# Causal attention: sums over tokens with whole fp32 probabilities, projected after the sum

## The reference

```python
x = _L0_conv_ref(x, ...)                       # attention without mask, added to x
t = _to_tokens(x)                              # (4, 1024, 64)
t = t + _L1_attn_ref(_ln_t(t), ...)            # causal attention, 8 heads of width 64
t = t + _L1_ffn_ref(_ln_t(t), ...)             # batch norm and a recurrence over tokens

def _L1_attn_ref(x, Wq, Wk, Wv, Wo):
    ...
    scores = jnp.einsum('bhqd,bhkd->bhqk', q, k) / D ** 0.5
    scores = jnp.where(causal[None, None], NEG_INF, scores)
    attn = jax.nn.softmax(scores, axis=-1)
    out = jnp.einsum('bhqk,bhkd->bhqd', attn, v)
    out = out.transpose(0, 2, 1, 3).reshape(B, N, H * D)
    return out @ Wo
```

## Time and profile before

| | |
|---|---|
| median of 3 runs | 571.24 us |
| the runs | 571.98, 571.24, 567.42 us |
| span of the profiled execution, first to last instruction | 567.0 us |
| mean granted TensorE clock | 0.974 of full speed |

### The profile page before, as it was taken

How to read it: one execution, slowest core, us unless ns; L and a number is a source line. 1 busy time by engine, 2 the same in 40 slices (tenths; PEclk the granted TensorE clock), 3 DMA queues, 4 the chain that set the end, 5 groups by cost and what they waited for, 6 DMA issues and landing times.

```text
span 567.0 us, 16744 instructions
## 1 busy us (share of the span) xinstructions
PE 490.0 (86%) x6771; PEld 323.0 (57%) x6771; DVE 398.8 (70%) x909; ACT 429.3 (76%) x832; POOL 424.4 (75%) x463
## 2 busy tenths in 40 slices
PE   4699978988799998889999988998999999787783
PEld 1277655655565755565666756565666766564431
DVE  5878888767678786576767676766767786328757
ACT  3488867866778878587888878787888878785593
POOL 3867965857988797968788797899788799985002
PEclk9999999989999999799999999999999999998698
DMA  9100000000000000000000000000000000000001
GB/s 230 68 3 2 2 20 1 4 1 3 1 22 2 3 3 2 3 1 21 2 3 2 4 3 1 21 3 1 1 3 3 2 3 2 2 2 2 0 2 74
DMA packets 3580, 7.46 MB, mean 13 GB/s; under 512 B 1168, under 2 KB 1456, under 8 KB 3376
## 3 DMA queue, kind: packets, MB, share of 16 engines
q1 hardware_dynamic: 3056, 5.34, 3.5%
q10 hardware_dynamic: 448, 1.05, 0.6%
HBM read 4.22 MB, written 1.05 MB: 9 GB/s over the span
## 4 chain that ended last, share of the span: by engine, by line
PE 45%; DVE 22%; POOL 17%; ACT 9%; issue 6%; DMA 1%; DVEq 0%; SPq 0%; POOLq 0%; ACTq 0%
POOL probs_low L1250 10%; PE bank L537 9%; DVE attn_partial_max L903 7%; ACT probs_high L779 6%; PE bank L497 6%; PE bank L570 5%; PE bank L574 4%; DVE conv_partial_max L897 3%; PE bank L578 3%; PE bank L576 3%; PE bank L455 2%; PE bank L522 2%; PE bank L483 2%; PE bank L456 2%; POOL tokens L1260 2%
## 5 line engine op out<-in xcount | busy, mean ns | idle before, releaser
L1250 POOL TENSOR_TENSOR probs_low<-probs,probs_high 128x512 f16<-128x512 f32 x288 | 327.6, 1158 | 77.5 <-ACT probs_high L779 76.7
L775 ACT ACTIVATE probs<-bank 128x512 f32<-128x512 f32 x352 | 214.7, 611 | 84.2 <-PE bank L537 69.0
L903 DVE TENSOR_REDUCE attn_partial_max<-bank 128x1 f32<-128x512 f32 (+2 forms) x288 | 185.3, 685 | 99.5 <-PE bank L497 99.0
L779 ACT ACTIVATE probs_high<-bank 128x512 f16<-128x512 f32 x288 | 176.8, 614 | 0.0
L574 PEld LDWEIGHTS bank<-values_high,probs_high 128*128 128x128 f16 x1152 | 105.7, 98 | 74.2 <-issue 35.8
L574 PE MATMUL bank<-values_high,probs_high 128*128 128x65 f16 x1152 | 128.8, 196 | 15.5 <-POOL probs_low L1250 11.4
L576 PE MATMUL bank<-values_low,probs_high 128*128 128x64 f16 x1152 | 127.6, 194 | 0.0
L578 PE MATMUL bank<-values_high,probs_low 128*128 128x65 f16 x1152 | 127.1, 194 | 0.0
L576 PEld LDWEIGHTS bank<-values_low,probs_high 128*128 128x128 f16 x1152 | 106.9, 99 | 3.2
L578 PEld LDWEIGHTS bank<-values_high,probs_low 128*128 128x128 f16 x1152 | 107.2, 98 | 0.0
L570 PE MATMUL bank<-values,probs 128*128 128x65 f32 x512 | 71.7, 278 | 0.8 <-POOL probs_low L1250 0.8
(11 more groups left out here) (192 smaller groups left out, 708.9 us busy)
## 6 DMA issues: line engine op xcount, KB each, us to landing
x_channels<-in_x_cm SPq DMA_DIRECT2D x6, 256.0 KB, 7.6
tokens<-in_x_tm SPq DMA_DIRECT2D x1, 1024.0 KB, 10.4
out<-ln_channels SPq DMA_DIRECT2D x4, 256.0 KB, 2.0
attn_weights<-in_attn_w ACTq DMA_DIRECT2D x1, 512.0 KB, 6.2
attn_keys_split<-attn_keys_high SPq DMA_DIRECT2D x4, 128.0 KB, 2.3
attn_keys_split<-attn_keys_low SPq DMA_DIRECT2D x4, 128.0 KB, 2.4
queries_high<-minus_max_rows SPq DMA_DIRECT2D x32, 2.0 KB
x_channels<-in_x_cm ACTq DMA_DIRECT2D x2, 128.0 KB, 3.2
```

The lines of the kernel that those rows point to most:

```text
L775: ins = nc.scalar.activation(e32[:, i % E_RING, :], o[:], ACT.Exp, scale=scale)
L779: ins = nc.scalar.activation(p_hi[:, i % P_RING, :], o[:], ACT.Exp, scale=scale)
L903: nc.vector.reduce_max(dst, o[:].rearrange("p (n w) -> p n w", n=n), AX).then_inc(s_prep_used, 1)
L1250: nc.gpsimd.tensor_tensor(out=p_lo[:, i % P_RING, :], in0=e32[:, i % E_RING, :], in1=p_hi[:, i % P_RING, :], op=ALU.subtract).then_inc(s_r ...
```

## The change

In the causal attention the order of the products is turned. The sum over keys is taken first, of the normalised tokens themselves (`xh`, 64 channels) and not of projected values. The tokens are now the stationary operand (128 keys by 64 channels) and the probabilities the moving one, 512 columns of fp32 at a time (`pe_sums`). The two heads of a pair write the two halves of one bank's partitions, that is of the array's columns. All attention items stay whole (`SPLIT_PAIRS` is empty), so the fp16 exponential and GpSimd's subtraction are gone from the causal stage.

When a half (512 queries of both heads) is closed, ScalarE writes the sums as fp16 (`act_sums`), VectorE the low rest (`dve_sums`), and the sums are projected by new auxiliary steps `outputs`, one per head and half, twelve products each. The denominators come out of the same products through a column of the value matrix that picks the constant channel 0. The `values` steps go.

The causal mask of the scores is no longer added by TensorE. GpSimd sets the masked probabilities to zero with a select, on both heads at once (`pool_mask`), 8 selects per unit. The mask of the row maxima stays on TensorE, as products over 64 rows. The layer-norm step of a batch (`pool_ln1`) also writes an fp16 high and low part, and several slot numbers move, because the outputs of a unit come later.

```diff
+SPLIT_PAIRS = ()
-ATTN_MAXT_SLOT, ATTN_VALUES_SLOTS = -4, (-2, 2)
+ATTN_MAXT_SLOT, OUTPUT_SLOTS, LAST_OUTPUT_SLOTS = -4, (12, 16, 24, 28), (12, 14, 24, 25)
...
+        def sums_bank(c):
+            return OT[1 - c]
...
+        def pe_mask(blocks, opens):
+
+            for half in range(2):
+                for r in range(2):
+                    nc.tensor.matmul(blocks[r], masks[rows(r), half, 0, :], masks[rows(r), half, 1, :],
+                                     start=opens and half == 0, stop=False, skip_group_check=True)
...
+        def pe_sums(i):
+
+            v = unit_of(i)
+            b = batch_of(v)
+            if not whole(i):
+                nc.tensor.wait_ge(s_rest, rests(i + 1))
+            elif diagonals(i):
+                nc.tensor.wait_ge(s_masked, masked(i))
+            else:
+                nc.tensor.wait_ge(s_probs, i + 2)
+            last = [None, None]
+            for j, t0, tiles, at in runs_of(i):
+                c = t0 // TPC
+                opens = (v, c) not in OPENED
+                if opens:
+                    OPENED.add((v, c))
+                    if v > B:
+                        nc.tensor.wait_ge(s_sums, 2 * (v - B - 1) + c + 1)
...
+                if whole(i):
+                    products = ((xh[b % 2][:, j, 0, :], e32, E_RING),)
...
+                for n, (x, p, ring) in enumerate(products):
+                    for r in range(2):
+                        last[r] = nc.tensor.matmul(sums_bank(c)[rows(r), cols], x, p[:, (i + r) % ring, src],
+                                                   start=opens and n == 0, stop=n == len(products) - 1,
+                                                   skip_group_check=True)
...
+            elif what == "outputs":
+                n, r = k // 2, k % 2
+                h = 2 * (n // NC % PAIRS) + r
+                nc.tensor.wait_ge(s_sums, n + 1)
                 for t in range(TPC):
...
+                    o, cols = bank[:, t * PO:(t + 1) * PO], slice(t * P, (t + 1) * P)
+                    hi, lo = o_hi[n % 2][rows(r), cols], o_lo[n % 2][rows(r), cols]
+                    nc.tensor.matmul(o, hi, pr_hi[rows(r), h, :], start=True, stop=False, skip_group_check=True)
+                    nc.tensor.matmul(o[:, 0:C], hi, pr_lo[rows(r), h, :], start=False, stop=False,
+                                     skip_group_check=True)
+                    ins = nc.tensor.matmul(o, lo, pr_hi[rows(r), h, :], start=False, stop=True,
+                                           skip_group_check=True)
...
+        def act_sums(n):
+
+            v, c = B + n // NC, n % NC
+            nc.scalar.wait_ge(s_values, closed_by(v, c) + 1)
+            if n >= 2:
+                nc.scalar.wait_ge(s_aux, AUX_OF["outputs", 2 * (n - 2) + 1] + 1)
+            nc.scalar.activation(o_hi[n % 2][:], sums_bank(c)[:], ACT.Copy).then_inc(s_sums_cast, 1)
...
+        def dve_sums(n):
+
+            nc.vector.wait_ge(s_sums_cast, n + 1)
+            nc.vector.tensor_tensor(out=o_lo[n % 2][:], in0=sums_bank(n % NC)[:], in1=o_hi[n % 2][:],
+                                    op=ALU.subtract).then_inc(s_sums, 1)
...
+        def pool_mask(i):
+
+            nc.gpsimd.wait_ge(s_probs, i + 2)
+            for at in diagonals(i):
+                e = e32[:, i % E_RING:i % E_RING + 2, at * P:(at + 1) * P]
+                nc.gpsimd.affine_select(out=e, in_=e, pattern=[[0, 2], [1, P]], compare_op=ALU.is_ge, fill=0.0, base=0,
+                                        channel_multiplier=-1).then_inc(s_masked, 1)
```

More of the change, by code:

```diff
@@ L28 @@
 LAG = 6
-CONV_WHOLE, ATTN_WHOLE = 4, 6
+CONV_WHOLE = 4
+SPLIT_PAIRS = ()
 LN_EPS = 1e-5
@@ L123, in runs_of, with diagonals, masked @@
     return [(n % NT, n // NT * TPC, TPC, 0)] if unit_of(i) < B else ATTN_RUNS[n // 2]
[L126 to L140, removed]
 def whole(i):
     n = i - first_slot(unit_of(i))
-    period = CONV_WHOLE if unit_of(i) < B else ATTN_WHOLE
-    return n % period == period - 1
+    return n % CONV_WHOLE == CONV_WHOLE - 1 if unit_of(i) < B else n // 2 not in SPLIT_PAIRS
+def diagonals(i):
+    return [at for j, t0, _, at in runs_of(i) if j == t0] if unit_of(i) >= B else []
+def masked(i):
+    return sum(len(diagonals(x)) for x in range(B * CONV_ITEMS, i + 1, 2))
 def rests(i):
@@ L188 @@
        for c, s in enumerate(QUERY_SLOTS_1 if v == B else QUERY_SLOTS)]
-    + [(first_slot(v) + s, 1, "values", 2 * v + c) for v in range(B, UNITS)
-       for c, s in enumerate(ATTN_VALUES_SLOTS)]
+    + [(g, 1, "outputs", 4 * (v - B) + k) for v in range(B, UNITS) for k, g in enumerate(output_slots(v))]
     + [(g, 2, "matrix", k) for k, g in enumerate(MATRIX_SLOTS)]
@@ L471, in pe_conv_prep @@
                              start=True, stop=True).then_inc(s_prep, 1)
+        def pe_mask(blocks, opens):
[3 more added lines that the diff above has]
+                                     start=opens and half == 0, stop=False, skip_group_check=True)
         def pe_max_masks(m):
             _, v, k = PREPS[m]
+            if v == B and k == 0:
+                nc.tensor.wait_ge(s_masks, 32)
             for r in range(2):
                 pe_wait_bank(BANK_HAD["prep", m + r])
[L478 to L482, removed]
[L483 to L485 removed]
+            ends = [(at + tiles) * P for t, j0, tiles, at in ATTN_MAXES[k // 2][0] if j0 + tiles - 1 == t]
+            for n, end in enumerate(ends):
+                pe_mask([prep_bank(m + r)[:, end - P:end] for r in range(2)], n == 0)
         def pe_maxes(m):
@@ L513, in pe_conv_scores @@
                              start=True, stop=True).then_inc(s_scores, 1)
-        def pe_score_masks(i):
-            nc.tensor.wait_ge(s_probs, i + 2 - ST_RING)
-            for r in range(2):
-                opened = False
-                for j, t0, tiles, at in runs_of(i):
-                    if j == t0:
-                        nc.tensor.matmul(ST[(i + r) % ST_RING][:, at * P:(at + 1) * P], identbf[:],
-                                         masks[:, 0, :], start=not opened, stop=False, skip_group_check=True)
-                        opened = True
         def pe_scores(i):
@@ L1359, in _ @@
             sp.dma_start(gbt[:], gb).then_inc(s_ffn, 16)
+            sp.wait_ge(s_init, 2)
+            for r in range(2):
+                sp.dma_start(masks[rows(r), 1, :, :], masks[rows(1 - r), 0, :, :]).then_inc(s_masks, 16)
             for m, (_, _, what, k) in enumerate(AUXES):
```

250 lines of the change are left out of this document (132 added, 118 removed).

## The result

The changed kernel takes 563.21 us (median of 4 runs, 562.46 to 564.71) against 570.74 us (4 runs, 567.42 to 571.98): a ratio of 0.988, 95% interval 0.985 to 0.992. It is 1.2% faster. The forecast was 593 us and slower: the sign is wrong. The time lies between the likeliest case and the first rival (554 us), and inside the stated range only because that range was drawn to take in this rival. The profiled execution took 564.71 us with a span of 562.8, so what lies around a span is 1.9 us; its mean granted clock is 0.961.

What follows compares the result with a forecast made beforehand. TensorE (45% of the chain) was to bound the kernel, its sums deciding: span 567.0 + 18 (1.1 us more in each of 16 units) + 3.5 = 588.5, median 4.2 above, so 593 us; range 543 to 618.

Steps and rivals of the forecast that it cites:

- the likeliest case: Causal stage: a single-run slot's sums cost 1.29 us on TensorE, time 593 us; chance 0.47.
- the first rival: Causal sums: the two heads overlap wholly, 0.86 us a single-run slot, 554 us and faster; chance 0.33.
- The price of the sums: TensorE's four fp32 records per single-run slot: taken as 1.29 us, between 0.86 (whole overlap) and 1.72 (none).
- three records deep: Sums of a slot: only the middle two of four records overlap, starts 0, 0.43, 0.43, 0.86, so 1.29 us.
- VectorE's waits: Outputs in slots 6, 10 and 12 wait for `sums_low` or `queries_low`, some 0.3 to 0.8 us.
- clean unit: Causal unit with nothing extra: nine slots, 16.48 + 9.90 = 26.4 us forecast.
- What else was to be hidden: `pool_ln1`'s added passes on GpSimd: nothing, unless selects behind them are late by more than three slots.
- Keys steps and statistics: Key steps and layer-norm statistics on VectorE: 1.0 us a unit, of which a third shows, 26.4 to 26.7.
- Off the path: ScalarE and GpSimd have ample room; their waits on TensorE go, and selects have three slots before their sums.
- the lower bound by size: GpSimd's select has no row: between half a `probs_low` (0.58 us) and a whole one (1.16), taken as 0.73.
- Start and end of the stage: Outside the units: +3 us for a cast, subtraction and two outputs steps at the end, +0.5 for memsets.
- 644: Causal sums: the column halves don't overlap at all, 1.72 us a slot, 644 us; chance 0.13.

Runs made afterwards that it cites:

- the single-head run: Changed kernel with head 1's sums left out, all but the first product of each half; 560.16 us, ratio 0.983.
- the layout that avoids most of it: Changed kernel with only the slots of queries and outputs steps moved; 536.25 us, ratio 0.940.
- the split pairs: Four of nine pairs as three fp16 products, against the 527.05 us kernel with steps re-laid, layer norm cut up, keys and later steps moved; 543.37 us.
- the layer norm in pieces: Changed kernel with GpSimd's layer-norm step cut into six pieces and its unread fp16 halves left out; 557.75 us, ratio 0.977.
- the keys moved: Changed kernel with keys steps of batches 2 and 3 and the later layer's steps in slots 0 and 2; 558.58 us, ratio 0.979.

## Why the prediction was wrong, point by point

*The price of the sums* is the step that failed. The prediction took 1.29 us, "three records deep", between bounds of 0.86 and 1.72. Measured is 0.48 for a pair of records, so 0.96 a slot; 1.01 to the next step's start with the change of shape in it, and 1.01 also for slots with two runs (1.08 and 1.18 forecast). The reason given was that starts in the listing are in program order and that head 1 stands behind head 0's second record. The trace has two starts together and then two; with the single-head run, that is one record of each head. What in the chip lets them pair is not shown here. The bounds were right to 0.2 us: 0.86 and 1.72 against 1.01 and 1.91, these with the change of shape.

By the Trainium skill, "TensorE: Matmul & The Clock Gate", section "Part 3: Packing small matmuls", products are first-in first-out in start and end. The listing shows no order among heads, so the rule itself stays unrefuted; what the prediction drew from it, that head 1 must wait for head 0's second record, is refuted by 1.01 against 1.91 us.

The Trainium skill, "TensorEngine Tiling (Array Packing)", "Key Properties", has tiles work independently, and the page's table under "Theoretical Speedup" up to twofold for 64 columns. The runs agree: 1.91 over 1.01 is 1.9.

*VectorE's waits* were right in place and size. Slots 6, 10 and 12 wait for what was named. By the starts of the maxima (L506), slot 6 took 3.36 us (forecast 3.42), and slots 10 and 12 together 6.41 (2.93 + 3.55). TensorE's idle time there is 1.9 us a unit, and the layout that avoids most of it saves 1.9. From slot 4's maxima to the next unit's the clean unit is 24.0, the first rival's figure to the tenth; that is not luck, since the five slots from slot 12's maxima on took 11.70 us where the rival had 11.59.

*What else was to be hidden.* `pool_ln1` was put at nothing "unless selects behind them are late by more than three slots". They were: its 8.3 us, with the add behind it 8.9, are more than three slots of 2.7. The clause named the right condition and didn't work it out, though `pool_ln1`'s passes were in the code; in one block, with the fp16 halves that nothing reads, it costs 5.5 us. Keys steps and statistics were given 0.3 us a unit as a third of their time on VectorE; the later layer's steps had no term. Both wait in bank 7 as well, and behind the longest stops the clock falls. Together the long units make the mean 1.3 us a unit above the clean 24.0. The kernel before had six such units, and the prediction put what they add down to GpSimd, by the 26.7 us that weight loads waited; the same view has TensorE's products waiting only 8.2 us for `probs_low`, so how much of it was GpSimd's is not shown.

*Off the path*, right: ScalarE's and GpSimd's waits are gone but for those behind `pool_ln1`, the masks of two heads overlap, outputs products are 0.03 us apart. A select is 0.406 us, below the lower bound by size (0.58); nothing hung on it.

*The sum.* Forecast 593. Clean unit 26.4 to 24.0 and 0.3 to 1.3 above it: -2.4 and +1.0, times 16, is -22. Start and end of the stage, +3.5 forecast: the first transpose is 1.9 us later than before and what follows the last 1.9 shorter, so -3.5. The median stands 0.4 above the profiled span and not 4.2: -4. That is 563. The same corrections to the first rival: 554 + 16 - 3.5 - 4 = 562.5. Its mechanism is the one that holds, with the disturbances too small.

## What to carry to other kernels

Where a price has no row and its two bounds give opposite signs, the case has to be called even, not by an argument on program order: 0.43 us per slot lay between 554 and 593 us, and as much again between 593 and 644. Work that is off the path on average has to be set against the few slots of cover that it has where it is one block in an engine's order; that was wrong for `pool_ln1` and again for the split pairs. And once every product is paid for, look at which step's reader stands at the end of another engine's slot: moving five steps of a unit by a slot or two gained 27 us, more than three times what the change itself did.

## What the runs showed of the hardware

- Two fp32 products of 128 rows by 64 columns, in different halves of the columns, run at the price of one: 1.01 us for 512 moving columns with two heads, 1.01 with one head alone, 1.91 with two heads of 128 columns each. All three hold the change of shape behind them.
- Waits of TensorE of 4.5, 2.0 and 1.9 us were each followed by a stretch at a lower granted clock (3 us stretches at 0.70, 0.50 and 0.57). With the stop gone the clock stayed at 1.00 in the same place (the layer norm in pieces), and with shorter waits too (the keys moved).
- A select of 128x256 fp32 on GpSimd is 0.406 us, where the add of 128x256 that the prediction took for it is 0.729.
